# Per-row scale columns of two row tiles computed together on VectorE, in a gated cross-attention and bit-quantised FFN kernel

## The chip, the cores and the metric

The kernel runs on one core of a Trainium2 chip. The metric is the time of one execution on the device in microseconds (us), smaller is better. The profile's times are counted from the start of the execution's span.

## The reference

The input x has 32 batches of 224 rows of 512 elements, 7168 rows in all. Two gated residual blocks follow each other:

```python
x = x + tanh(g_xattn[0]) * xattn(layernorm(x), ctx, pad_mask, Wq, Wkv)
x = x + tanh(g_ffn[0]) * ffn(layernorm(x), w1, b1, w2, b2)

def rmsnorm(x):      return x * rsqrt(mean(x * x) + 1e-5)
def act_quant(x):    # per row
    scale = 127.0 / clip(max(abs(x)), 1e-5)
    return clip(round(x * scale), -128, 127) / scale
def weight_quant(w): # ternary, one scale for the whole matrix
    scale = 1.0 / clip(mean(abs(w)), 1e-5)
    return clip(round(w * scale), -1, 1) / scale
def bitlinear(x, w, b): return act_quant(rmsnorm(x)) @ weight_quant(w).T + b
ffn: bitlinear(gelu(bitlinear(x, w1, b1)), w2, b2)     # 512 -> 2048 -> 512
```

Each row of a layer's input so needs a handful of single numbers: its rms factor, its peak, the step with which it is quantised, and the factor that undoes the step after the matmul.

## The kernel before

The kernel has two stages in one launch. The first, until about 1587 us, is the cross-attention; it writes its rows to HBM. The second is the FFN, and only it is touched.

The second stage works on 56 row tiles of 128 rows (a row on each partition). Its steps are numbered s = -2 to 57, and a step works on several tiles at once: tile s goes through the first matmul, the GELU and its own quantisation (this is called **hidden**: its middle layer, 2048 columns in `hid`), tile s - 1 through the second matmul, and tile s + 2 is loaded, normalised and quantised (**ahead**: the input tile, 512 columns in `xc`). Steps 0 to 53 have both hidden and ahead. Steps -2 and -1 have ahead only, 54 and 55 hidden only. Steps 4 to 51 are a loop with four steps to a turn. Each engine has its own fixed order of instructions inside a step, and semaphores join them.

VectorE's order in a step: `L1007` (four pieces, matmul result times a column plus bias into `hid`), `L1011` and `L1014` (transposed tiles out of PSUM to bf16), `L1018`, `L1020`, `L1022` (mean and variance of tile s + 2), `L1026` (peak of `hid`, HMAX), `L1029` (HMS, from the sum of squares of ScalarE), `L1034` (peak of `xc`, XMAX), then eight small instructions on one column each, `L1039` to `L1060`, and `L1065`, which quantises `xc` into `xq`. The next step starts with `L1007` again.

The small instructions write columns of `cols`. For hidden they are HCLIP (L1039), HINV (L1048), HDEQ (L1053) and HS (L1055), for ahead XCLIP (L1044), XINV (L1051), XS (L1058) and XDEQ (L1060). Each `own_cols` wait makes VectorE wait for its own earlier result.

GpSimd's order in a step: `L928` and `L930` (x1 of tile s + 2 from x and the attention rows), `L916` (the final sum of tile s - 2), `L935` and `L938` (FAC, the factor of tile s + 2), `L943` (`xc`), `L947` (HR, the rms factor of tile s, after L1029), `L951` (x1 plus the bias of the second layer). In the trace L951 of one step is directly followed by L928, L930 and L916 of the next.

ScalarE's order: `L968` (GELU, four pieces), `L971` (transposed tile out of PSUM), `L976` (sum of squares), `L982` (the second matmul's result), `L985` (quantises `hid` with HS, waits for `t_hs`). TensorE's: `L1086` (first matmul, 16 matmuls), `L1094` (transposes `xq`, waits for `t_xq`), `L1103` (transposes the quantised hidden tile, waits for L985), `L1115` (second matmul, waits for L1014). SP issues the loads of a tile after `t_x1` (L930) and the store of a result after `t_yo` (L916).

Of the kernel before, what the change touches and what calls it, by code (L numbers as in the profile page):

```python
# [8 lines left out]
ALU = mybir.AluOpType  # L9
# [5 lines left out]
CLIP = 1e-5  # L15
LEVELS = 127.0
# [7 lines left out]
def gated_cross_attention_bit_ffn(nc, x, ctx_t, mask_row, mask_col, g_xattn, g_ffn,  # L24
# [32 lines left out]
    with outer:  # L57
        def sem(name):
            return outer.enter_context(nc.semaphore(name))

        def allocator(stack):
            return lambda name, shape, dt=F32: stack.enter_context(nc.sbuf_tensor(name, shape, dt))
# [11 lines left out]
        sb = allocator(outer)  # L74
        gates = sb("gates", [128, 2])
# [8 lines left out]
        w_mean = sb("w_mean", [128, 2])  # L84
# [6 lines left out]
        sb = allocator(phase_a)  # L91
# [724 lines left out]
        sb = allocator(phase_b)  # L816
        w1_q = sb("w1_q", [128, DC, F], BF16)
        w2_q = sb("w2_q", [128, FC, D], BF16)
        round_col = sb("round_col", [128, 2])
        w_gated = sb("w_gated", [128, 1])  # L820
        b1_row = sb("b1_row", [128, F])
        b2_row = sb("b2_row", [128, D])
        b2_gated = sb("b2_gated", [128, D])
# [2 lines left out]
        x1b = sb("x1b", [128, 2, D])  # L826
        xc = sb("xc", [128, 2, D])
        x_st, x_mv2 = sb("x_st", [128, 6]), sb("x_mv2", [128, 2, 2])
        cols = sb("cols", [128, 2, 16])
        xq = sb("xq", [128, 2, D])  # L830
        xq_t = sb("xq_t", [128, 2, DC * 128], BF16)
        hid = sb("hid", [128, 2, F])
# [1 line left out]
        hq = sb("hq", [128, 2, F])  # L834
        hq_t = sb("hq_t", [128, 2, FC * 128], BF16)
        yo = sb("yo", [128, 2, D])
        (NEGM, FVAR, FAC, XMAX, XCLIP, XINV, XS, XDEQ, HSS, HMS, HR, HMAX, HCLIP, HINV, HS, HDEQ) = range(16)


        halves = psum[:].bitcast(F16)  # L840
# [7 lines left out]
        b_const, b_wg, b_b2 = sem("b_const"), sem("b_wg"), sem("b_b2")  # L848
# [4 lines left out]
        t_g, t_ss, t_ms, t_hr, t_hs = sem("t_g"), sem("t_ss"), sem("t_ms"), sem("t_hr"), sem("t_hs")  # L853
        t_hq, t_ht, t_ha, t_hd = sem("t_hq"), sem("t_ht"), sem("t_ha"), sem("t_hd")
        t_y, t_ye, t_yo = sem("t_y"), sem("t_ye"), sem("t_yo")
        own_ab, own_fac, own_st, own_cols = sem("own_ab"), sem("own_fac"), sem("own_st"), sem("own_cols")

        def exists(k):
            return not isinstance(k, int) or 0 <= k < NT

        def is_step(s, n):
            return isinstance(s, int) and s == n

        def run_steps(eng, step):
            full = (NT - 2) // NX
            for s in range(-2, NX):
                step(s, s, 0)
            with eng.Fori(1, full) as u:
                for j in range(NX):
                    step(eng.snap(u * NX + j), j, u)  # L870
            for s in range(full * NX, NT + 2):
                step(s, s - full * NX, full)

        with nc.Block() as block:
# [80 lines left out]
            @block.scalar  # L955
            def _(act):
                act.wait_ge(b_const, 2)
                w2_flat = w2_q[:].rearrange("p c n -> p (c n)")

                def step(s, j, u):  # L960
                    c = cols[:, j % 2, :]
                    if is_step(s, 0):
                        act.activation(w2_flat, w_raw[:, DC * F:], ACT.Copy, bias=-ROUND).then_inc(b_wq2, 1)
                    if exists(s):
                        for i in range(FS):
                            seg = hid[:, j % 2, BANK * i:BANK * i + BANK]
                            act.wait_ge(t_he, FS * s + (i + 1))
                            act.activation(seg, seg, ACT.Gelu).then_inc(t_g, 1)  # L968
                    if exists(s - 1):
                        act.wait_ge(t_ht, 2 * s)  # L970
                        act.activation(hq_t[:, (j - 1) % 2, F // 2:], ps_ht[1], ACT.Copy, bias=-HALF_BIAS).then_inc(t_ha, 1)  # L971
                    if exists(s):
                        act.wait_ge(t_g, FS * s + FS)
                        if exists(s - 1):
                            act.wait_ge(t_ss, s)
                        act.activation(junk[:], hid[:, j % 2, :], ACT.Square, accum_out=c[:, HSS:HSS + 1]).then_inc(t_ss, 1)  # L976
                    if exists(s - 1):
                        p = (j - 1) % 2
                        act.wait_ge(t_y, s)
                        if exists(s - 3):  # L980
                            act.wait_ge(b_st[p], 16 * (2 * u + (j - 3) // 2 + 1))
                        act.activation(yo[:, p, :], ps_y, ACT.Copy, scale=cols[:, p, HDEQ:HDEQ + 1]).then_inc(t_ye, 1)  # L982
                    if exists(s):
                        act.wait_ge(t_hs, s + 1)
                        act.activation(hq[:, j % 2, :], hid[:, j % 2, :], ACT.Identity, scale=c[:, HS:HS + 1],  # L985
                                       bias=round_col[:, 1:2]).then_inc(t_hq, 1)

                run_steps(act, step)

            @block.vector  # L990
            def _(dve):
                dve.tensor_scalar(w1_q[:].rearrange("p c n -> p (c n)"), stage, ROUND, 1.0, ALU.subtract, ALU.mult).then_inc(b_wq1, 1)
                dve.tensor_tensor(w_gated[:], w_mean[:, 1:2], gates[:, 1:2], ALU.mult).then_inc(b_wg, 1)
                dve.wait_ge(b_wg, 1)

                def step(s, j, u):
                    c, slot = cols[:, j % 2, :], (j + 2) % NX
                    hidden, ahead = exists(s), exists(s + 2)
                    if is_step(s, 0):
                        dve.wait_ge(b_bias, 32)  # L1000
                    if hidden:
                        if exists(s - 2):
                            dve.wait_ge(t_hq, s - 1)
                        for i in range(FS):
                            dve.wait_ge(t_h, FS * s + (i + 1))
                            n = slice(BANK * i, BANK * i + BANK)
# [17 lines left out]
                    if hidden:  # L1024
# [2 lines left out]
                                          apply_absolute_value=True).then_inc(own_cols, 1)  # L1027
                        dve.wait_ge(t_ss, s + 1)
                        dve.tensor_scalar(c[:, HMS:HMS + 1], c[:, HSS:HSS + 1], 1.0 / F, RMS_EPS, ALU.mult, ALU.add).then_inc(t_ms, 1)  # L1029
                    h = 1 if hidden else 0  # L1030
                    x = 1 if ahead else 0
                    if ahead:
                        dve.wait_ge(t_xc, s + 3)
                        dve.tensor_reduce(c[:, XMAX:XMAX + 1], xc[:, j % 2, :], AX.X, ALU.max,  # L1034
                                          apply_absolute_value=True).then_inc(own_cols, 1)
                    if hidden:
                        dve.wait_ge(t_hr, s + 1)
                        dve.wait_ge(own_cols, h)
                        dve.tensor_scalar(c[:, HCLIP:HCLIP + 1], c[:, HMAX:HMAX + 1], c[:, HR:HR + 1], CLIP,  # L1039
                                          ALU.mult, ALU.max).then_inc(own_cols, 1)  # L1040
                    if ahead:
                        dve.wait_ge(t_fac, s + 3)
                        dve.wait_ge(own_cols, h + x)
                        dve.tensor_scalar(c[:, XCLIP:XCLIP + 1], c[:, XMAX:XMAX + 1], c[:, FAC:FAC + 1], CLIP,  # L1044
                                          ALU.mult, ALU.max).then_inc(own_cols, 1)
                    if hidden:
                        dve.wait_ge(own_cols, h + x + h)
                        dve.reciprocal(c[:, HINV:HINV + 1], c[:, HCLIP:HCLIP + 1]).then_inc(own_cols, 1)  # L1048
                    if ahead:
                        dve.wait_ge(own_cols, 2 * (h + x))  # L1050
                        dve.reciprocal(c[:, XINV:XINV + 1], c[:, XCLIP:XCLIP + 1]).then_inc(own_cols, 1)  # L1051
                    if hidden:
                        dve.tensor_scalar(c[:, HDEQ:HDEQ + 1], c[:, HCLIP:HCLIP + 1], 1.0 / LEVELS, w_gated[:], ALU.mult, ALU.mult)  # L1053
                        dve.wait_ge(own_cols, 2 * (h + x) + h)
                        dve.tensor_scalar(c[:, HS:HS + 1], c[:, HINV:HINV + 1], LEVELS, c[:, HR:HR + 1], ALU.mult, ALU.mult).then_inc(t_hs, 1)  # L1055
                    if ahead:
                        dve.wait_ge(own_cols, 3 * (h + x))
                        dve.tensor_scalar(c[:, XS:XS + 1], c[:, XINV:XINV + 1], LEVELS, c[:, FAC:FAC + 1],  # L1058
                                          ALU.mult, ALU.mult).then_inc(own_cols, 1)
                        dve.tensor_scalar(c[:, XDEQ:XDEQ + 1], c[:, XCLIP:XCLIP + 1], 1.0 / LEVELS, w_mean[:, 0:1],  # L1060
                                          ALU.mult, ALU.mult).then_inc(own_cols, 1)
                        if exists(s):
                            dve.wait_ge(t_xt, s + 1)
                        dve.wait_ge(own_cols, 3 * (h + x) + 1)
                        dve.tensor_scalar(xq[:, j % 2, :], xc[:, j % 2, :], c[:, XS:XS + 1], ROUND_HALF, ALU.mult, ALU.add).then_inc(t_xq, 1)  # L1065
                        dve.wait_ge(own_cols, 3 * (h + x) + 2)
                    if hidden or ahead:
                        dve.sem_clear(own_cols)

                run_steps(dve, step)  # L1070

            @block.tensor
# [76 lines left out]
```

## Time and profile before

| | |
|---|---|
| median of 3 runs | 2128.5 us (2127.22 to 2129.57) |
| the profiled execution | 2131.0 us |
| its span in the trace | 2129.2 us |
| TensorE busy | 1971.3 us, 93% |
| VectorE busy | 1236.9 us, 58% |
| ScalarE busy | 1060.9 us, 50% |
| GpSimd busy | 565.8 us, 27% |
| mean granted clock of TensorE | 0.981 |

The shares are means over both stages. In the page's 40 slices TensorE shows nines nearly throughout the first stage and eights in the last ten slices, where VectorE shows nines. What bounds the second stage has to be read from that stretch alone.

### The profile page before, as it was taken

To read this page: it belongs to the slowest core of one execution; us is meant where nothing else is said; L and a number is where in the kernel's file an instruction comes from. 1 tells how busy PE (TensorE), PEld (TensorE's weight loads), DVE (VectorE), ACT (ScalarE), POOL (GpSimd) and SP (SyncE) were. 2 spreads that over 40 slices of the span, in tenths; PEclk is the share of its full clock that TensorE was granted. 3 is DMA by queue.
4 is the path that set the end of the run, shared out by engine and by line. 5 is a ranking of instruction groups with operands and counts; after the bars stand their busy time and mean duration, and the time that the engine had idled before them with its cause. 6 is when DMAs were issued, how large, how long until landed. Compare 5 with 4: busy or idle time off the path is not lost. (4 is left out here: it accounts for less than half of the span.)

```text
span 2129.2 us, 47929 instructions
## 1 busy us (share of the span) xinstructions
PE 1971.3 (93%) x17116; PEld 1501.0 (70%) x17173; DVE 1236.9 (58%) x2371; ACT 1060.9 (50%) x1826; POOL 565.8 (27%) x619
## 2 busy tenths in 40 slices
PE   5999999999997999999999899999977888888887
PEld 4888888788886878888888688888763444444443
DVE  5455445444443444444544244444348999999996
ACT  2444433334333433333444244333346888888887
POOL 1111111111111111111111011111106777777774
PEclk9999999999998999999999899999998999999999
DMA  6000001021001003000000200001032222222221
GB/s 256 27 26 26 26 26 30 24 78 48 28 26 48 26 6 96 32 26 26 26 26 26 79 27 26 26 26 40 15 96 70 84 89 89 89 89 86 81 84 55
DMA packets 51968, 112.19 MB, mean 53 GB/s; under 512 B 5047, under 2 KB 5047, under 8 KB 51288
## 3 DMA queue, kind: packets, MB, share of 16 engines
q1 hardware_dynamic: 51928, 111.67, 15.9%
q8 instruction: 23, 0.38, 0.1%
q14 instruction: 17, 0.14, 0.0%
HBM read 93.36 MB, written 29.43 MB: 58 GB/s over the span
## 5 line engine op out<-in xcount | busy, mean ns | idle before, releaser
L316 POOL TENSOR_TENSOR y_l<-y,y_h 128x750 fp32r<-128x750 f32 x96 | 172.9, 1802 | 818.5 <-ACT y_h L378 818.1
L502 DVE TENSOR_REDUCE nmax<-psum 112x1 f32<-112x750 f32 x248 | 233.0, 939 | 164.3 <-PE psum L627 161.5
L400 ACT ACTIVATE prob<-psum,nmax 112x750 f32<-112x750 f32 x248 | 219.8, 886 | 92.8 <-DVE nmax L502 88.0
L1115 PE MATMUL psum<-w_q,hq_t 128*128 128x512 bf16 x841 | 194.5, 384 | 61.9 <-DVE hq_t L1014 61.9
L627 PE MATMUL psum<-y_h,wkv_h 128*128 128x512 f32 x756 | 208.4, 357 | 42.3 <-DVE wkv_l L465 14.0
L627 PE MATMUL psum<-wkv_h,y_h 128*125 128x512 f32 x558 | 226.6, 406 | 0.0
L721 PE MATMUL psum<-ident,prob 112*125 112x112 f32 x1488 | 214.9, 281 | 9.3 <-ACT prob_t L391 6.4
L627 PE MATMUL psum<-wkv_l,y_h 128*125 128x512 f32 x558 | 220.5, 395 | 0.0
L627 PE MATMUL psum<-wkv_h,y_l 128*125 128x512 f32 x558 | 220.4, 395 | 0.0
L1086 PE MATMUL psum<-w_q,xq_t 128*128 128x512 bf16 x895 | 204.6, 382 | 2.3 <-DVE xq_t L1011 2.3
L721 PEld LDWEIGHTS psum<-ident,prob 112*125 112x125 f32 x1488 | 181.3, 188 | 35.6 <-issue 22.8
L391 ACT ACTIVATE prob_t<-psum 125x336 f32<-125x336 f32 x248 | 111.2, 448 | 190.5 <-PE psum L721 190.4
L627 PE MATMUL psum<-y_l,wkv_h 128*128 128x512 f32 x756 | 196.6, 342 | 0.0
L627 PE MATMUL psum<-y_h,wkv_l 128*128 128x512 f32 x756 | 194.9, 340 | 0.0
L1115 PEld LDWEIGHTS psum<-w_q,hq_t 128*128 128x128 bf16 x896 | 84.5, 98 | 154.1 <-issue 63.8
L424 ACT ACTIVATE v<-psum 125x512 f32<-125x512 f32 x93 | 55.6, 597 | 247.8 <-PE psum L627 247.8
L524 DVE COPY prob_t<-psum 125x336 f32<-125x336 f32 x248 | 124.9, 504 | 75.4 <-PE psum L721 74.5
L1086 PEld LDWEIGHTS psum<-w_q,xq_t 128*128 128x128 bf16 x896 | 88.1, 98 | 109.4 <-issue 4.2
L627 PEld LDWEIGHTS psum<-y_h,wkv_h 128*128 128x128 f32 x756 | 116.7, 194 | 60.0 <-issue 38.3
L1007 DVE SCALAR_TENSOR_TENSOR hid<-psum,cols,b_row 128x512 f32<-128x512 f32 x224 | 152.7, 738 | 5.5 <-PE psum L1086 5.0
L321 POOL TENSOR_SCALAR x_var<-x_mv 56x1 f32<-56x1 f32 x31 | 5.7, 183 | 513.8 <-DVE x_mv L485 513.8
L627 PE MATMUL psum<-k_h,q_h 128*112 128x512 f32 x496 | 137.2, 357 | 4.4 <-issue 4.4
(122 smaller groups left out, 3651.0 us busy)
## 6 DMA issues: line engine op xcount, KB each, us to landing
y<-in_ctx_t SPq DMA_DIRECT2D x32, 1125.0 KB, 5.3
xb<-in_x SPq DMA_DIRECT2D x56, 256.0 KB, 2.7
ab<-attn_rows SPq DMA_DIRECT2D x56, 256.0 KB, 2.9
out_rows<-yo SPq DMA_DIRECT2D x56, 256.0 KB, 2.0
attn_rows<-vmean_rows SPq DMA_DIRECT2D x32, 336.0 KB
w_raw<-in_w_t SPq DMA_DIRECT2D x2, 4096.0 KB, 16.6
xa<-in_x SPq DMA_DIRECT2D x32, 112.0 KB
attn_rows<-attn SPq DMA_DIRECT2D x31, 112.0 KB
```

The costliest lines, as they stand in the source:

```text
L316: pool.tensor_tensor(y_l[:, c, :], y[:, c, :], y_h[:, c, :].bitcast(F32), ALU.subtract).then_inc(a_yl, 1)
L321: pool.tensor_scalar(x_var[:], x_mv[:, 1:2], 1.0, LN_EPS, ALU.mult, ALU.add).then_inc(own_var, 1)
L391: act.activation(prob_t[:, i % 2, 0:MH, :].rearrange("p j n -> p (j n)"), ps_pt[0], ACT.Copy).then_inc(p.pa, 1)
L400: act.activation(prob[:, i % 3, :], ps_score[i % 2][0:RP, :], ACT.Exp, bias=nmax[:, i:i + 1], accum_out=den[:, i:i + 1]).then_inc(p.exp, 1)
L424: act.activation(v[:, j, :], ps_v[0], ACT.Copy).then_inc(a_va, 1)
L502: dve.tensor_reduce(nmax[:, i:i + 1], ps_score[i % 2][0:RP, :], AX.X, ALU.max, negate=True).then_inc(p.max, 1)
L524: dve.tensor_copy(prob_t[:, i % 2, MH:MJ, :].rearrange("p j n -> p (j n)"), ps_pt[1]).then_inc(p.pd, 1)
L627: mm = pe.matmul(out[:, s0:s1], a, r[:, s0:s1], start=first and n == 0, stop=last_ and n == 2)
L721: mm = pe.transpose(ps_pt[hf][:, RP * j:RP * j + RP], prob[:, m % 3, MC * jj:MC * jj + MC], ident[0:RP, 0:RP])
L1007: dve.scalar_tensor_tensor(out=hid[:, j % 2, n], in0=psum[:, i, :], scalar=c[:, XDEQ:XDEQ + 1], in1=b1_row[:, n], op0=ALU.mult, op1=ALU.ad ...
L1086: mm = pe.matmul(psum[:, i, :], xq_t[:, j % 2, 128 * c:128 * c + 128], w1_q[:, c, BANK * i:BANK * i + BANK], start=(c == 0), stop=(c == DC ...
L1115: mm = pe.matmul(ps_y, hq_t[:, p, 128 * c:128 * c + 128], w2_q[:, c, :], start=(c == 0), stop=(c == FC - 1))
```

## The change

The small instructions of hidden and ahead are merged: the columns of both are laid side by side in `cols`, and five instructions work on two columns where eight worked on one. Their form changes with it. The factor of each row was a pointer scalar of a tensor_scalar; now products of two columns are a tensor_tensor with two inputs in SBUF. In steps with only one of the two, the same five instructions run on one column. The semaphore `t_hs` now counts every such step, so ScalarE waits for s + 3. The text calls the five RAW, QUANT, INV, DEQ and STEP, after what they write.

```diff
-        w_gated = sb("w_gated", [128, 1])
-        cols = sb("cols", [128, 2, 16])
+        cols = sb("cols", [128, 2, 18])
...
+        NEGM, FVAR, HSS, HMS = range(4)
+        HR, FAC, HMAX, XMAX, HS, XS, HDEQ, XDEQ = range(4, 12)
+        RMS, PEAK, STEP, DEQ, RAW, QUANT, INV = 4, 6, 8, 10, 12, 14, 16
+        w_pair = sb("w_pair", [128, 2])
...
-                        act.wait_ge(t_hs, s + 1)
+                        act.wait_ge(t_hs, s + 3)
...
-                dve.tensor_tensor(w_gated[:], w_mean[:, 1:2], gates[:, 1:2], ALU.mult).then_inc(b_wg, 1)
-                dve.wait_ge(b_wg, 1)
+                dve.tensor_tensor(w_pair[:, 0:1], w_mean[:, 1:2], gates[:, 1:2], ALU.mult).then_inc(b_wg, 1)
+                dve.tensor_copy(w_pair[:, 1:2], w_mean[:, 0:1]).then_inc(b_wg, 1)
+                dve.wait_ge(b_wg, 2)
...
                     if hidden:
                         dve.wait_ge(t_hr, s + 1)
-                        dve.wait_ge(own_cols, h)
-                        dve.tensor_scalar(c[:, HCLIP:HCLIP + 1], c[:, HMAX:HMAX + 1], c[:, HR:HR + 1], CLIP,
-                                          ALU.mult, ALU.max).then_inc(own_cols, 1)
                     if ahead:
                         dve.wait_ge(t_fac, s + 3)
...
+                    if hidden or ahead:
+                        h, x = 0 if hidden else 1, 2 if ahead else 1
+                        n = x - h
+                        dve.wait_ge(own_cols, n)
+                        dve.tensor_tensor(c[:, RAW + h:RAW + x], c[:, PEAK + h:PEAK + x], c[:, RMS + h:RMS + x],
+                                          ALU.mult).then_inc(own_cols, 1)
+                        dve.wait_ge(own_cols, n + 1)
+                        dve.tensor_scalar(c[:, QUANT + h:QUANT + x], c[:, RAW + h:RAW + x], CLIP, 1.0 / LEVELS,
+                                          ALU.max, ALU.mult).then_inc(own_cols, 1)
+                        dve.wait_ge(own_cols, n + 2)
+                        dve.reciprocal(c[:, INV + h:INV + x], c[:, QUANT + h:QUANT + x]).then_inc(own_cols, 1)
+                        dve.tensor_tensor(c[:, DEQ + h:DEQ + x], c[:, QUANT + h:QUANT + x], w_pair[:, h:x],
+                                          ALU.mult).then_inc(own_cols, 1)
+                        dve.wait_ge(own_cols, n + 3)
+                        dve.tensor_tensor(c[:, STEP + h:STEP + x], c[:, INV + h:INV + x], c[:, RMS + h:RMS + x],
+                                          ALU.mult).then_inc(t_hs, 1)
                     if ahead:
...
                         if exists(s):
                             dve.wait_ge(t_xt, s + 1)
-                        dve.wait_ge(own_cols, 3 * (h + x) + 1)
+                        dve.wait_ge(t_hs, s + 3)
                         dve.tensor_scalar(xq[:, j % 2, :], xc[:, j % 2, :], c[:, XS:XS + 1], ROUND_HALF, ALU.mult, ALU.add).then_inc(t_xq, 1)
-                        dve.wait_ge(own_cols, 3 * (h + x) + 2)
                     if hidden or ahead:
+                        dve.wait_ge(own_cols, n + 4)
                         dve.sem_clear(own_cols)
```

The other seven small instructions of before (L1044 to L1060) go in the same way as L1039.

## Rows read from the trace of the kernel before

**Rows 1.** Busy time of each engine in the even stretch of the second stage.
```profile
1700.00:2100.00 400.00, 350.30 (x2245) 187.25 (x2287) 391.40 (x924) 337.92 (x397) 288.85 (x352) 1.00 0.25 85
```

**Rows 2.** Timeline of TensorE: start, length, line, shape, count, [idle before, releaser].
```profile
1903.57 3.40 PE L1115 MATMUL psum<-w_q,hq_t 128*128 128x512 bf16 x15 [1.38 <-DVE hq_t L1014]
1906.81 3.62 PE L1086 MATMUL psum<-w_q,xq_t 128*128 128x512 bf16 x16
...
1912.60 3.40 PE L1115 MATMUL psum<-w_q,hq_t 128*128 128x512 bf16 x15 [1.06 <-DVE hq_t L1014]
```

**Rows 3.** Timeline of VectorE around the edited piece of one step.
```profile
1906.44 0.68 DVE L1034 TENSOR_REDUCE cols<-xc 128x1 f32<-128x512 f32 x1
1907.19 0.21 DVE L1039 TENSOR_SCALAR cols<-cols 128x1 f32<-128x1 f32 x1
...
1908.18 0.49 DVE L1065 TENSOR_SCALAR xq<-xc,cols 128x512 f32<-128x512 f32 x1
1908.60 1.40 DVE L1007 SCALAR_TENSOR_TENSOR hid<-psum,cols,b_row 128x512 f32<-128x512 f32 x2
```

**Rows 4.** Timelines of GpSimd and VectorE in steps -2 and -1.
```profile
1599.23 1.26 POOL L930 TENSOR_TENSOR x<-xb,ab 128x512 f32<-128x512 f32 x1
...
1605.51 0.69 POOL L928 TENSOR_SCALAR ab<-ab,gates 128x512 f32<-128x512 f32 x1 [0.23 <-POOL b_gated L909]
...
1600.00 0.78 DVE L1065 TENSOR_SCALAR xq<-xc,cols 128x512 f32<-128x512 f32 x1
...
1604.65 0.69 DVE L1034 TENSOR_REDUCE cols<-xc 128x1 f32<-128x512 f32 x1 [1.74 <-POOL xc L943]
1605.44 0.21 DVE L1044 TENSOR_SCALAR cols<-cols 128x1 f32<-128x1 f32 x1
1605.69 0.16 DVE L1051 RECIPROCAL cols<-cols 128x1 f32<-128x1 f32 x1
...
1606.14 0.48 DVE L1065 TENSOR_SCALAR xq<-xc,cols 128x512 f32<-128x512 f32 x1
```

**Rows 5.** Groups of small VectorE forms: count, busy us, mean ns, idle before.
```profile
L487 DVE TENSOR_TENSOR x_keep<-x_rstd,mcol 56x1 f32<-56x1 f32 x31 | 4.7, 152 | 36.3 <-POOL x_rstd L323 36.3
...
L1029 DVE TENSOR_SCALAR cols<-cols 128x1 f32<-128x1 f32 x56 | 8.1, 144 | 1.0 <-ACT junk L976 1.0
```

**Rows 6.** Timeline of GpSimd in the same step as rows 3.
```profile
1906.60 0.55 POOL L947 TENSOR_TENSOR cols<-cols,half 128x1 f32<-128x1 f32 x1 [0.69 <-DVE cols L1029]
1907.12 1.27 POOL L951 TENSOR_TENSOR x1b<-x,b_gated 128x512 f32<-128x512 f32 x1
1908.37 0.86 POOL L928 TENSOR_SCALAR ab<-ab,gates 128x512 f32<-128x512 f32 x1
1909.31 1.28 POOL L930 TENSOR_TENSOR x<-xb,ab 128x512 f32<-128x512 f32 x1
1910.55 1.30 POOL L916 TENSOR_TENSOR yo<-yo,x1b 128x512 f32<-128x512 f32 x1
```

**Rows 7.** First stage: L465 on VectorE (timeline, group) and GpSimd's timeline.
```profile
11.87 2.06 DVE L465 TENSOR_TENSOR wkv_l<-w_raw,wkv_h 128x1536 fp32r<-128x1536 f32 x1 [11.75 <-ACT wkv_h L360]
...
L465 DVE TENSOR_TENSOR wkv_l<-w_raw,wkv_h 128x1536 fp32r<-128x1536 f32 x2 | 3.7, 1901 | 11.7 <-ACT wkv_h L360 11.7
...
8.81 3.50 POOL L316 TENSOR_TENSOR y_l<-y,y_h 128x750 fp32r<-128x750 f32 x2
```

**Rows 8.** Timelines of VectorE and GpSimd at the second stage's start.
```profile
1589.21 4.43 DVE L992 TENSOR_SCALAR w_q<-w_raw 128x8192 bf16<-128x8192 f32 x1 [2.57 <-PEq L221]
1593.55 0.15 DVE L993 TENSOR_TENSOR w_gated<-w_mean,gates 128x1 f32<-128x1 f32 x1
...
1592.89 1.31 POOL L928 TENSOR_SCALAR ab<-ab,gates 128x512 f32<-128x512 f32 x1 [3.60 <-DMA ab<-attn_rows]
```

**Rows 9.** TensorE after a wait in the first stage, and the granted clock (last but two).
```profile
418.73 4.43 PE L796 MATMUL psum<-wv,y_sum 128*8 128x512 f32 x6 [2.03 <-DVE y_sum L603]
...
419.00:423.00 4.00, 4.00 (x6) 0.50 (x4) 0.00 (x0) 0.00 (x0) 0.00 (x0) 0.57 0.00 0
```

More of the change, by code:

```diff
@@ L836, in gated_cross_attention_bit_ffn @@
         yo = sb("yo", [128, 2, D])
-        (NEGM, FVAR, FAC, XMAX, XCLIP, XINV, XS, XDEQ, HSS, HMS, HR, HMAX, HCLIP, HINV, HS, HDEQ) = range(16)
+        NEGM, FVAR, HSS, HMS = range(4)
+        HR, FAC, HMAX, XMAX, HS, XS, HDEQ, XDEQ = range(4, 12)
+        RMS, PEAK, STEP, DEQ, RAW, QUANT, INV = 4, 6, 8, 10, 12, 14, 16
+        w_pair = sb("w_pair", [128, 2])
         halves = psum[:].bitcast(F16)
@@ L1029, in step @@
                         dve.tensor_scalar(c[:, HMS:HMS + 1], c[:, HSS:HSS + 1], 1.0 / F, RMS_EPS, ALU.mult, ALU.add).then_inc(t_ms, 1)
-                    h = 1 if hidden else 0
-                    x = 1 if ahead else 0
                     if ahead:
@@ L1037, in step @@
                         dve.wait_ge(t_hr, s + 1)
-                        dve.wait_ge(own_cols, h)
-                        dve.tensor_scalar(c[:, HCLIP:HCLIP + 1], c[:, HMAX:HMAX + 1], c[:, HR:HR + 1], CLIP,
-                                          ALU.mult, ALU.max).then_inc(own_cols, 1)
                     if ahead:
                         dve.wait_ge(t_fac, s + 3)
-                        dve.wait_ge(own_cols, h + x)
-                        dve.tensor_scalar(c[:, XCLIP:XCLIP + 1], c[:, XMAX:XMAX + 1], c[:, FAC:FAC + 1], CLIP,
-                                          ALU.mult, ALU.max).then_inc(own_cols, 1)
@@ L1046, in step @@
-                    if hidden:
-                        dve.wait_ge(own_cols, h + x + h)
-                        dve.reciprocal(c[:, HINV:HINV + 1], c[:, HCLIP:HCLIP + 1]).then_inc(own_cols, 1)
-                    if ahead:
[L1050 to L1061, printed above, removed]
+                    if hidden or ahead:
[14 more added lines that the diff above has]
+                                          ALU.mult).then_inc(t_hs, 1)
```

## The prediction, made before the change was run

> **What bounds the kernel now.** I read the page first for the shares, then the busy times of the long even stretch, then the timelines of single engines through one step, and last the odd places where a VectorE and a GpSimd instruction meet. In the even stretch from 1700 to 2100 us VectorE is busy 391.4 of 400 us and TensorE 350.3 [rows 1], at full granted clock. The second stage repeats every 9.03 us, as the two starts of the L1115 group show (1903.57 and 1912.60), and each time TensorE waits 1.06 to 1.38 us for VectorE's L1014 [rows 2]. So VectorE's chain of instructions sets the period, and what the change does to it counts 54 times (the steps that have both a hidden tile and a tile two ahead), with two half steps at each end.
>
> All times below without the 19 in front are of the step shown: 7.19 is 1907.19. The piece that is edited runs from L1039 at 7.19 to the start of L1065 at 8.18: eight small instructions in 0.99 us, 0.12 each [rows 3]. They need not wait for each other, since hidden and ahead alternate. L1065 writes xq and ends at 8.67; L1007, the next step's first, starts at 8.60.
>
> **The change on an idle chip.** It removes eight small instructions and adds five: RAW, QUANT, INV, DEQ and STEP. DEQ and INV follow QUANT without a wait between them; all the others wait for the one before. In the half steps a waiting instruction starts 0.04 after the end of what it waits for (L1044 ends at 5.65, L1051 starts at 5.69), and 0.10 after where the instruction has two waits (L1034 ends at 5.34, L1044 starts at 5.44) [rows 4]. The small forms take 0.144 (two immediates) and 0.152 (tensor_tensor) [rows 5], a reciprocal 0.16 [rows 4]. RAW starts 0.10 after the end of L1034, which is 7.12, so at 7.22 instead of 7.19 (it has three waits, one more than that pair of rows shows, so up to another 0.06 is possible). Then RAW to QUANT 0.19, QUANT to INV 0.18, INV to STEP 0.20, and STEP to L1065 0.25 (two waits): L1065 would start at 8.04 to 8.08 instead of 8.18, 0.10 to 0.14 earlier. TensorE could follow that only in part: the L1086 group ends at 10.43 [rows 2], and the fourth piece of L1007, 0.66 us apart from its neighbours, starts at 8.60 + 1.98 = 10.58 [rows 3]. That is 0.1 of slack once the handoff is paid. The wait that ScalarE's L985 has on STEP would end where it ends now. No DMA and no queue is moved: SP waits for t_x1 and t_yo, both GpSimd's. The 0.1 per step would be 6 us in all. I don't believe in it, for the reason that follows.
>
> **What GpSimd does meanwhile.** As soon as L947 is through, GpSimd starts L951, a tensor_tensor on 512 columns, at 7.12 and is in it until 8.39; then L928 (8.37), L930 (9.31) and L916 (10.55) follow without a pause [rows 6]. The whole edited piece lies beside L951, and now costs nothing of it. But some VectorE instructions can't run beside a GpSimd one. In step -2, L1065 starts at 1600.00 while GpSimd's L930 (1599.23 for 1.26) is in flight, and takes 0.78; in step -1 it takes 0.48 [rows 4]. The long one ends 0.29 after L930's end at 1600.49, so it was held until GpSimd had finished, and only then read its columns. Of the 0.48, then, 0.20 go by before the columns and 0.28 over them. The same is seen with a tensor_tensor of two SBUF inputs: the first L465 starts at 11.87 while L316 runs until 8.81 + 3.50 = 12.31, and takes 2.06, where its twin takes 2 x 1.901 - 2.06 = 1.74; it ends 1.62 after L316, which is its 1536 columns at 1.05 ns [rows 7]. Of its time 0.13 go by before the columns.
>
> In the shown step L1065 ends at 8.67, and 8.39 + 0.28 is 8.67 [rows 3, 6]: today it is already held, by a hair, to the end of L951. GpSimd is held in turn: L928 takes 0.86 instead of the 0.69 of [rows 4], ending 0.56 after L1065's end. So moving L1065's start forward gains nothing; its end stays at 8.67 unless L951 ends earlier, and L951 hangs on L1029 and L947, which the edit leaves alone. The gain above falls to zero.
>
> **What the new instructions cost there.** The old small ones have one column, a pointer scalar or immediates, and one tensor input; L1039 shows 0.21 beside L951 and the eight fit into 0.99, so there is no hold. The new RAW, DEQ and STEP are tensor_tensor with two SBUF inputs, like L465. RAW would start at 7.22 and want its columns at 7.35; L951 has been in since 7.12, so RAW is held until 8.39 and ends at 8.41. What that hold is worth for two columns no row shows. From below it is nothing: L993, one column, two SBUF inputs, took 0.152 at 1593.55, while L928, held by L992 until 1593.64, ended at 1594.20, the same 0.56 after [rows 8]. But L993 began while VectorE itself still had what L928 waited for. From above it is L465's full hold. I take the hold, since the kind is L465's and the overlap here is clean: GpSimd is in first by 0.10.
>
> QUANT has one tensor input, but two columns where all the old ones had one. L1065's 512 columns go by in 0.28, 0.55 ns each against 1.05 for L465, so that form reads two columns at once, and it was held. [...] Bounds: not held like L1029 (0.144), or held like L1065. I take held. [...]
>
> The order of events, with each side starting as today after what it follows: QUANT starts at 8.45, but L928 has been in since 8.37 and needs 0.69, so until 9.06; QUANT ends at 9.08. INV runs from 9.12 to 9.28. DEQ starts at 9.20 and wants its columns at 9.33; L930 starts 0.08 after L928, at 9.14, and is in until 10.41; DEQ ends at 10.43. STEP starts 0.08 before that (as neighbours do), wants its columns at 10.48, and L916 starts at 10.37 and, by the same 0.14 that L928 shows (0.69 - 0.56), at 10.51: STEP just gets in and ends at 10.50. L1065 starts at 10.60 and is held by L916 to 10.37 + 1.28 = 11.65; it ends at 11.93 instead of 8.67. That is **3.26 us per step**. If STEP comes too late by the 0.03, it ends at 11.67, L1065 starts at 11.77 and ends at 12.25: 3.58. If DEQ comes before L930, STEP is held instead, and the end is the same to 0.1. I take 3.3. The period becomes 12.3 us. After L1065 everything follows as today: L985 starts near 10.55 instead of 7.99 and still ends before L1014; TensorE has its L1115 and L1086 done early and waits for xq, then for L1014.
>
> Sum: 54 x 3.3 = 178 us. The half steps at the start add some 0.9 (RAW held to 1600.49 in step -2), the two last ones at most a L951 and most of a L916 each, together 3.5, since STEP there feeds L985 directly. 182 us on the profiled execution's 2131.0 is 2313. That execution is 2.5 us above the median of 2128.5, so the forecast is **2310 us**.
>
> **Rivals.** (a) QUANT is not held, the tensor_tensors are. Then QUANT ends at 8.60, INV at 8.80, DEQ is held by L928 to 9.08, STEP gets in before L930 and ends at 9.15, and L1065, started at 9.26, is held by L930 to 10.41 and ends at 10.69: 2.0 per step, 54 x 2.0 + 4 = 112, so 2241. For it: every old small tensor_scalar ran free. Against: none had two columns.
>
> (b) Only QUANT is held, the small tensor_tensors are not (L993's reading). QUANT ends at 8.41, STEP at 8.80, L1065 starts at 8.91, gets in before L930 and ends at 9.39: 0.72 per step, 39 us, 2167.
>
> (c) Not slower: nothing as small as two columns is held, as L993 was not. Then L1065 is ready at 8.08 and still held to 8.39 by L951: the end stays 8.67 and the time 2128. It decides if the two-column instructions show 0.15 and not 1.2 beside L951.
>
> (d) Faster: nothing is held, L1065 neither, and the 0.1 of TensorE's slack is taken: 2122. Against it stands L1065's end at L951's end + 0.28. [...]
>
> (e) TensorE loses its clock. [...]
>
> **How the numbers follow.** Forecast 0.60, (a) 0.14, (b) 0.08, (c) 0.07, (d) 0.03, (e) 0.06, anything else 0.02. The forecast's own range is 2290 to 2345: 3.0 to 3.9 per step. The range 2160 to 2350 takes in (a) and (b) and leaves out (c), (d) and (e), 0.18. What a measurement can tell from no change is 0.2%, 4.3 us: faster 0.03, same 0.07, slower 0.90.
>
> **What would show it.** Right: the first tensor_tensor takes about 1.2 us and ends with L951; L1065 ends near a GpSimd end + 0.28 or runs after L916; the period is near 12.3; GpSimd's own times stay. If QUANT shows 0.15 it is (a); if the tensor_tensors show 0.15 it is (b) or (c). Wrong in size: the 0.03 us races at STEP and DEQ, and GpSimd starting in another order once VectorE is late.

## The result and the profile after

The changed kernel takes **2300.6 us** (median of 4 runs, 2298.6 to 2303.8); the kernel before took 2127.9 us (4 runs) beside it. The ratio is 1.082, with a 95% interval of 1.0806 to 1.0834. The forecast was 2310, the range 2160 to 2350. The change makes the kernel 8% slower.

Lines have moved: L1034 is now L1036, L1065 (xq) L1062, L1007 L1011, L985 L988; on GpSimd L947 is L950, L951 (x1b) L954, L928 L931, L930 L933, L916 L919. The five new instructions are RAW L1046, QUANT L1049, INV L1052, DEQ L1053 and STEP L1056.

The timeline of VectorE in one step of the changed kernel, with its next L1011, answers to [rows 3]:

```profile
1907.13 0.68 DVE L1036 TENSOR_REDUCE cols<-xc 128x1 f32<-128x512 f32 x1
1907.94 1.16 DVE L1046 TENSOR_TENSOR cols<-cols 128x2 f32<-128x2 f32 x1
1909.13 0.64 DVE L1049 TENSOR_SCALAR cols<-cols 128x2 f32<-128x2 f32 x1
1909.81 0.17 DVE L1052 RECIPROCAL cols<-cols 128x2 f32<-128x2 f32 x1
1909.89 1.22 DVE L1053 TENSOR_TENSOR cols<-cols,w_pair 128x2 f32<-128x2 f32 x1
1911.03 0.15 DVE L1056 TENSOR_TENSOR cols<-cols 128x2 f32<-128x2 f32 x1
1911.29 1.32 DVE L1062 TENSOR_SCALAR xq<-xc,cols 128x512 f32<-128x512 f32 x1
1912.53 2.71 DVE L1011 SCALAR_TENSOR_TENSOR hid<-psum,cols,b_row 128x512 f32<-128x512 f32 x4
```

And the timeline of GpSimd in the same step, to [rows 6]:

```profile
1907.30 0.55 POOL L950 TENSOR_TENSOR cols<-cols,half 128x1 f32<-128x1 f32 x1 [0.69 <-DVE cols L1033]
1907.81 1.27 POOL L954 TENSOR_TENSOR x1b<-x,b_gated 128x512 f32<-128x512 f32 x1
1909.06 0.69 POOL L931 TENSOR_SCALAR ab<-ab,gates 128x512 f32<-128x512 f32 x1
1909.83 1.26 POOL L933 TENSOR_TENSOR x<-xb,ab 128x512 f32<-128x512 f32 x1
1911.05 1.27 POOL L919 TENSOR_TENSOR yo<-yo,x1b 128x512 f32<-128x512 f32 x1
```

Read the two side by side, adding start and length. RAW ends at 9.10, x1b (L954) at 9.08. QUANT ends at 9.77, L931 at 9.75. DEQ ends at 11.11, L933 at 11.09. STEP gets in between L933 and L919 and takes its plain 0.15. xq ends at 12.61, 0.29 after L919's 12.32. Four of these six instructions (RAW, QUANT, DEQ and xq) end 0.02 or 0.29 after a GpSimd instruction, so most of their long durations must be waiting; the experiments below show it. No column of the view names GpSimd as the releaser: it isn't a semaphore that is waited for, and the time is booked as VectorE busy. So the page of the changed kernel shows VectorE busier, 1402.3 us against 1236.9, with fewer instructions, 2214 against 2371:

```profile
PE 2055.8 (89%) x17172; PEld 1515.9 (66%) x17173; DVE 1402.3 (61%) x2214; ACT 1081.7 (47%) x1826; POOL 554.4 (24%) x619
```

The groups of VectorE by shape in the second stage of the changed kernel (columns as in [rows 5]) show that this is so in all 54 steps with both halves:

```profile
L1062 DVE TENSOR_SCALAR xq<-xc,cols 128x512 f32<-128x512 f32 x56 | 71.6, 1279 | 5.9
L1053 DVE TENSOR_TENSOR cols<-cols,w_pair 128x2 f32<-128x2 f32 x54 | 65.1, 1205 | 0.0
L1046 DVE TENSOR_TENSOR cols<-cols 128x2 f32<-128x2 f32 x54 | 62.3, 1155 | 7.2
L1049 DVE TENSOR_SCALAR cols<-cols 128x2 f32<-128x2 f32 x54 | 35.2, 651 | 1.9
L1052 DVE RECIPROCAL cols<-cols 128x2 f32<-128x2 f32 x54 | 9.0, 166 | 1.8
L1056 DVE TENSOR_TENSOR cols<-cols 128x2 f32<-128x2 f32 x54 | 8.0, 148 | 0.0
```

The reciprocal is the only one of the five that is never held, and STEP arrives at the right moment. STEP can be held too: in step -1 of the run with half of x1b, below, it took 0.52 and ended 0.01 after GpSimd's instruction. Whether the reciprocal is free or only lucky in its moment, these rows alone don't say.

### The profile page after: what moved, and what is told of

Same layout as the page of the kernel before. It is cut to its first block and busy times, and to the rows that moved or that the text cites. A ratio compares the mean times of both kernels' runs of the same rounds, so it can differ in the third digit from the quotient of the medians.

```text
span 2302.0 us, 47774 instructions
## 1 busy us (share of the span) xinstructions
PE 2055.8 (89%) x17172; PEld 1515.9 (66%) x17173; DVE 1402.3 (61%) x2214; ACT 1081.7 (47%) x1826; POOL 554.4 (24%) x619
## 5 line engine op out<-in xcount | busy, mean ns | idle before, releaser
L1112 PE MATMUL psum<-w_q,hq_t 128*128 128x512 bf16 x896 | 258.7, 454 | 91.5 <-DVE hq_t L1018 91.5
L1112 PEld LDWEIGHTS psum<-w_q,hq_t 128*128 128x128 bf16 x896 | 97.5, 113 | 235.8 <-issue 175.4
L1083 PE MATMUL psum<-w_q,xq_t 128*128 128x512 bf16 x896 | 206.2, 384 | 3.2 <-DVE xq_t L1015 3.2
L988 ACT ACTIVATE hq<-hid,round_col,cols 128x2048 f32<-128x2048 f32 x56 | 117.3, 2095 | 101.2 <-DVE cols L1056 101.0
L1083 PEld LDWEIGHTS psum<-w_q,xq_t 128*128 128x128 bf16 x896 | 88.5, 99 | 111.6 <-issue 5.8
L1011 DVE SCALAR_TENSOR_TENSOR hid<-psum,cols,b_row 128x512 f32<-128x512 f32 x224 | 152.1, 737 | 0.2
L971 ACT ACTIVATE hid<-hid 128x512 f32<-128x512 f32 x224 | 139.8, 629 | 16.9 <-DVE hid L1011 12.2
```

Source lines behind the costliest of these rows:

```text
L1011: dve.scalar_tensor_tensor(out=hid[:, j % 2, n], in0=psum[:, i, :], scalar=c[:, XDEQ:XDEQ + 1], in1=b1_row[:, n], op0=ALU.mult, op1=ALU.ad ...
L1083: mm = pe.matmul(psum[:, i, :], xq_t[:, j % 2, 128 * c:128 * c + 128], w1_q[:, c, BANK * i:BANK * i + BANK], start=(c == 0), stop=(c == DC ...
L1112: mm = pe.matmul(ps_y, hq_t[:, p, 128 * c:128 * c + 128], w2_q[:, c, :], start=(c == 0), stop=(c == FC - 1))
```

## The experiments

In each diff the kernel it starts from is named. Between them these runs had 63 runs of the kernel before beside them, with medians of 2127.6, 2126.6 and 2126.5 us in the three sets.

**QUANT on one column at a time.** From the changed kernel:

```diff
-  dve.tensor_scalar(c[:, QUANT + h:QUANT + x], c[:, RAW + h:RAW + x], CLIP, 1.0 / LEVELS, ALU.max, ALU.mult).then_inc(own_cols, 1)
+  for i in range(h, x):
+      q = dve.tensor_scalar(c[:, QUANT + i:QUANT + i + 1], c[:, RAW + i:RAW + i + 1], CLIP, 1.0 / LEVELS, ALU.max, ALU.mult)
+  q.then_inc(own_cols, 1)
```

> Only QUANT is changed: two instructions on one column each in the place of one on two. Theory (hold: a VectorE instruction with two SBUF inputs, or with one SBUF input that can be split in two, waits until the GpSimd instruction in flight has ended): QUANT now shows 0.15 us, RAW stays near 1.15, DEQ is held by the short GpSimd L931 only, STEP gets in before L933, and xq ends with L933 instead of L919, so 2.0 us per step over the kernel before instead of 3.25: 2237 us. Rival (chain: the five are slow because each waits for the one before, whatever GpSimd does): one instruction more in the chain, so no faster than the changed kernel, 2300 us or a few more.

Measured: 2235.7 us, ratio 1.0507 (1.0491 to 1.0523). One instruction more makes the kernel 65 us faster, so the length of the chain is not what costs. The timeline of VectorE, with its x1b ending at 1913.74:

```profile
1912.60 1.16 DVE L1046 TENSOR_TENSOR cols<-cols 128x2 f32<-128x2 f32 x1
1913.79 0.21 DVE L1050 TENSOR_SCALAR cols<-cols 128x1 f32<-128x1 f32 x2
1914.04 0.17 DVE L1054 RECIPROCAL cols<-cols 128x2 f32<-128x2 f32 x1
```

The two one-column QUANTs run together in 0.21 while GpSimd's L931 is in flight (1913.71 to 1914.41); on two columns the same work took 0.64. The reciprocal on two columns lies wholly beside L931 too and takes its 0.17, so on two columns the tensor_scalar was held (0.64) and the reciprocal was not (0.17).

**All five on one column at a time.** From the changed kernel, each line of the five becomes a loop over the columns (ten instructions), for example:

```diff
-  dve.tensor_tensor(c[:, RAW + h:RAW + x], c[:, PEAK + h:PEAK + x], c[:, RMS + h:RMS + x], ALU.mult).then_inc(own_cols, 1)
+  for i in range(h, x):
+      dve.tensor_tensor(c[:, RAW + i:RAW + i + 1], c[:, PEAK + i:PEAK + i + 1], c[:, RMS + i:RMS + i + 1], ALU.mult).then_inc(own_cols, 1)
```

> The changed kernel with each of the five done on one column at a time (ten instructions), products still with two SBUF inputs. Theory (hold, whatever the number of columns): the first RAW is held about 1.15 us to the end of the GpSimd x1b instruction, QUANT runs free (one column can't be split), the first DEQ is held by the short GpSimd instruction; then the last STEP and GpSimd's next come to within 0.02 us of each other: 2236 if STEP is first, 2302 if not. Rival (one column is too little to be held, as L993 seemed to show): everything free and xq held to the end of x1b as before, 2128 to 2135.

Measured: 2235.0 us, ratio 1.0512 (1.0496 to 1.0528); the last STEP came in time. The two RAWs and the two QUANTs here, with x1b ending at 1909.85:

```profile
1908.71 1.23 DVE L1048 TENSOR_TENSOR cols<-cols 128x1 f32<-128x1 f32 x2
1909.90 0.22 DVE L1052 TENSOR_SCALAR cols<-cols 128x1 f32<-128x1 f32 x2
```

The first RAW waits for x1b and the second stands behind it. One column was enough for the hold with two SBUF inputs (1.23 for the two RAWs), and not with one (0.22 for the two QUANTs). The changed kernel shows it by itself in its two last steps, where only hidden is left and the same instruction has one column (the two steps are alike); its timelines of VectorE and GpSimd:

```profile
2274.88 1.21 DVE L1046 TENSOR_TENSOR cols<-cols 128x1 f32<-128x1 f32 x1 [0.66 <-POOL cols L950]
2276.12 0.15 DVE L1049 TENSOR_SCALAR cols<-cols 128x1 f32<-128x1 f32 x1
...
2274.81 1.26 POOL L954 TENSOR_TENSOR x1b<-x,b_gated 128x512 f32<-128x512 f32 x1
```

**Only QUANT left exposed.** From the changed kernel; peak and INV go to a free part of PSUM, a copy of w_pair too, so that each product has one input there:

```diff
+  pcols = psum[:, 7, 256:272].rearrange("p (a b) -> p a b", a=2)      # p = pcols[:, j % 2, :]
+  w_psum = psum[:, 7, 272:274]
+  dve.tensor_copy(w_psum, w_pair[:])
-  dve.tensor_tensor(c[:, RAW + h:RAW + x], c[:, PEAK + h:PEAK + x], c[:, RMS + h:RMS + x], ALU.mult)
+  dve.tensor_tensor(c[:, RAW + h:RAW + x], p[:, P_PEAK + h:P_PEAK + x], c[:, RMS + h:RMS + x], ALU.mult)
   dve.tensor_scalar(c[:, QUANT + h:QUANT + x], c[:, RAW + h:RAW + x], CLIP, 1.0 / LEVELS, ALU.max, ALU.mult)
-  dve.reciprocal(c[:, INV + h:INV + x], c[:, QUANT + h:QUANT + x])
+  dve.reciprocal(p[:, P_INV + h:P_INV + x], c[:, QUANT + h:QUANT + x])
```

DEQ and STEP change in the same way.

> The two-column chain in which only QUANT has its input and output in SBUF and two columns; each product has one of its inputs in PSUM. Theory (hold by the form that takes two columns at once): QUANT is held to the end of x1b and takes near 1.1 us, the others 0.15 to 0.2, xq starts 0.7 us later than before, gets in ahead of the next but one GpSimd instruction and ends 0.73 later per step: 2167 us. Rival (only two SBUF inputs are held): 2126, as with all in PSUM.

Measured: 2166.0 us, ratio 1.0185 (1.017 to 1.0201). GpSimd's x1b runs from 1907.00 to 1908.26 in this step of VectorE's timeline:

```profile
1907.13 0.16 DVE L1052 TENSOR_TENSOR cols<-psum,cols 128x2 f32<-128x2 f32 x1
1907.33 0.97 DVE L1055 TENSOR_SCALAR cols<-cols 128x2 f32<-128x2 f32 x1
1908.33 0.17 DVE L1058 RECIPROCAL psum<-cols 128x2 f32<-128x2 f32 x1
```

The product that was held for 1.16 takes 0.16 beside the same x1b, and QUANT takes the wait on itself. That is the price of QUANT alone, 39 us. It is also what rival (b) had worked out for a kernel in which only QUANT is held, 2167.

**None exposed.** The same, with RAW and QUANT in PSUM too (and w_pair back in SBUF, since DEQ's other input now lies in PSUM):

```diff
-  dve.tensor_scalar(c[:, QUANT + h:QUANT + x], c[:, RAW + h:RAW + x], CLIP, 1.0 / LEVELS, ALU.max, ALU.mult)
+  dve.tensor_scalar(p[:, P_QUANT + h:P_QUANT + x], p[:, P_RAW + h:P_RAW + x], CLIP, 1.0 / LEVELS, ALU.max, ALU.mult)
```

> The same five instructions on two columns with the same waits, but peak, RAW, QUANT and INV lie in a free part of PSUM, so none has two SBUF inputs or an SBUF input to split. Theory (hold): all five show 0.15 to 0.20 us, xq starts 0.1 us earlier than in the kernel before and is still held to the end of the GpSimd x1b instruction, so the period is 9.03 us again: 2128 us, within 3. Rival (chain): the five stay at about 3.2 us beyond before, 2300. Rival (the hold of xq is no hold but chance): xq ends 0.1 earlier and the time is 2122.

Measured: 2125.9 us, ratio 0.9995 (0.9986 to 1.0004). Same five instructions, same waits, same two columns, and 175 us less. Its timelines of VectorE and GpSimd:

```profile
1910.33 0.17 DVE L1049 TENSOR_TENSOR psum<-psum,cols 128x2 f32<-128x2 f32 x1
...
1911.21 0.54 DVE L1065 TENSOR_SCALAR xq<-xc,cols 128x512 f32<-128x512 f32 x1
...
1910.20 1.26 POOL L956 TENSOR_TENSOR x1b<-x,b_gated 128x512 f32<-128x512 f32 x1
```

xq starts 0.05 earlier in the step than in [rows 3] and takes 0.54 instead of 0.49: it ends at 11.75, where x1b's 11.46 + 0.28 says. The time gained ahead of it is gone in it, as the prediction said of the kernel before.

**x1b behind xq, in both kernels.** One wait of GpSimd moves, from both kernels:

```diff
-  pool.wait_ge(t_xq, s + 1)
+  if exists(s + 2):
+      pool.wait_ge(t_xq, s + 3)      # xq of this step
+  else:
+      pool.wait_ge(t_hs, s + 3)      # s + 1 in the kernel before
   ...
   pool.tensor_tensor(x1b[:, j % 2, :], x1[:, j % NX, :], b2_gated[:], ALU.add).then_inc(t_x1b, 1)
```

> The changed kernel with one wait of GpSimd moved: its x1b instruction, and with it the three that follow, waits until xq of this step is written (in the two last steps until STEP is). Nothing on VectorE is changed. Theory (hold): RAW, QUANT, DEQ and STEP show 0.15 us, xq shows 0.49 and ends 0.1 to 0.15 us earlier in the step than before, TensorE becomes the bound at a period near 8.93: 2122 us, between 2119 and 2127. Rival (chain): 2300, since VectorE's order and waits are the same. Rival (GpSimd late): the three GpSimd instructions now end 1.2 us later and hold up the next step's statistics, which would show as VectorE waiting for x1: over 2135.

> The kernel before with the same GpSimd wait moved. Theory (hold): only xq was held there, by 0.01 us, and nothing else of VectorE is touched, so the period stays 9.03: 2128 us within 2. It gives what the moved wait costs or gives by itself, to be taken off the run beside it. Rival: if the moved wait by itself helps, 2122 here too; if GpSimd comes late, over 2135.

Measured: the changed kernel with it 2123.0 us, ratio 0.9984 (0.9974 to 0.9993); the kernel before with it 2128.5, ratio 0.9998 (0.9989 to 1.0007). VectorE's timeline in the changed kernel with x1b late:

```profile
1909.32 0.68 DVE L1039 TENSOR_REDUCE cols<-xc 128x1 f32<-128x512 f32 x1
1910.13 0.16 DVE L1049 TENSOR_TENSOR cols<-cols 128x2 f32<-128x2 f32 x1
1910.33 0.17 DVE L1052 TENSOR_SCALAR cols<-cols 128x2 f32<-128x2 f32 x1
1910.53 0.17 DVE L1055 RECIPROCAL cols<-cols 128x2 f32<-128x2 f32 x1
1910.62 0.14 DVE L1056 TENSOR_TENSOR cols<-cols,w_pair 128x2 f32<-128x2 f32 x1
1910.73 0.16 DVE L1059 TENSOR_TENSOR cols<-cols 128x2 f32<-128x2 f32 x1
1911.00 0.49 DVE L1065 TENSOR_SCALAR xq<-xc,cols 128x512 f32<-128x512 f32 x1
```

Nothing of VectorE was edited, and everything is back to 0.14 to 0.17. The two together say that the change is worth some 4 to 5 us once GpSimd is out of its way, and that the moved wait alone is worth nothing. The period here is 8.95 instead of 9.02 us, which over 54 steps is 4 us. With both remedies the result should not be better than with one:

> Both remedies together: the five with PSUM inputs, and x1b after xq. Theory: neither is needed once the other is there, so the same as the changed kernel with x1b late, or 1 to 2 us slower, since the PSUM forms showed 0.17 to 0.18 instead of 0.15 to 0.17: 2123 to 2126. Rival (the remedies add up): under 2121.

Measured: 2123.4 us, ratio 0.9989 (0.998 to 0.9998), period 8.98. They don't add up.

**How long x1b is.** Two tests of the dose. From the changed kernel, x1b on half its columns (its other half is filled with zeros once, so this kernel leaves half of the residual out of its result):

```diff
-  pool.tensor_tensor(x1b[:, j % 2, :], x1[:, j % NX, :], b2_gated[:], ALU.add)
+  pool.tensor_tensor(x1b[:, j % 2, 0:D // 2], x1[:, j % NX, 0:D // 2], b2_gated[:, 0:D // 2], ALU.add)
```

> The changed kernel with x1b done on 256 of its 512 columns (the other half of the residual is left out of the result). Theory: RAW is held to an end that comes 0.57 us earlier (256 columns at 2.2 ns), and everything behind it, GpSimd's and VectorE's, moves with it: 2300.6 - 54 x 0.57 = 2270 us. Rival (the wait is for something else, and x1b's length is nothing to VectorE): 2300.

Measured: 2269.7 us, ratio 1.0676 (1.0659 to 1.0692), where 2270 was expected. The period fell by 0.54 and not by 0.57, to 11.73, so that the two agree to the microsecond is partly chance. VectorE's and GpSimd's timelines:

```profile
1904.45 0.62 DVE L1047 TENSOR_TENSOR cols<-cols 128x2 f32<-128x2 f32 x1
...
1904.32 0.72 POOL L955 TENSOR_TENSOR x1b<-x,b_gated 128x256 f32<-128x256 f32 x1
```

On the kernel before, the first try was to do x1b twice:

```diff
+  pool.tensor_tensor(x1b[:, j % 2, :], x1[:, j % NX, :], b2_gated[:], ALU.add).then_inc(own_fac, 1)
+  pool.wait_ge(own_fac, 1)
   pool.tensor_tensor(x1b[:, j % 2, :], x1[:, j % NX, :], b2_gated[:], ALU.add).then_inc(t_x1b, 1)
+  pool.sem_clear(own_fac)
```

> The kernel before with GpSimd's x1b instruction done twice in a row (the second writes the same again). Theory (xq of the kernel before is already held to the end of x1b): each step grows by the whole second instruction, 1.24 us, though GpSimd is busy only seven tenths of the time: 54 x 1.24 = 67, 2195 us. Rival (GpSimd's idle time is free; xq and x1b only happen to end in step): GpSimd has 1.6 us to spare ahead of the statistics, so 2128.

Measured: 2125.9 us, ratio 0.9995 (0.9985 to 1.0006). The expectation was wrong, and the rival's 2128 was right in number. The timelines of VectorE and GpSimd say why, and that the rival's reason doesn't follow from it:

```profile
1905.46 0.49 DVE L1068 TENSOR_SCALAR xq<-xc,cols 128x512 f32<-128x512 f32 x1
...
1904.40 1.27 POOL L951 TENSOR_TENSOR x1b<-x,b_gated 128x512 f32<-128x512 f32 x1
1905.75 1.35 POOL L953 TENSOR_TENSOR x1b<-x,b_gated 128x512 f32<-128x512 f32 x1
```

The second x1b waits for the first and starts 0.08 us after it. By then xq, already waiting, has gone in, and now it is GpSimd that is held, for 1.35 instead of 1.27. Here it is the instruction in flight that holds (xq 0.49 with the first x1b ended), and not the work that GpSimd has still to do. The test of the dose must move the end of the one in flight, so a small instruction was put ahead of it:

```diff
   pool.tensor_tensor(c[:, HR:HR + 1], c[:, HMS:HMS + 1], half[:], ALU.pow).then_inc(t_hr, 1)
+  pool.tensor_scalar(spare[:], ident[:], 1.0, 1.0, ALU.mult, ALU.mult).then_inc(own_fac, 1)
+  pool.wait_ge(own_fac, 1)
+  pool.sem_clear(own_fac)
```

> The kernel before with one small GpSimd instruction more (128 columns, into a spare tile) ahead of x1b, so that x1b starts and ends about 0.35 us later; unlike the doubled x1b, whose start fell behind xq's, x1b itself is still the one in flight when xq wants its columns. Theory (xq of the kernel before ends with x1b + 0.28): each step grows by 0.34, 54 x 0.34 = 18, 2145 us. Rival (xq isn't held in the kernel before, GpSimd's idle time covers it): 2127.

Measured: 2151.3 us, ratio 1.0116 (1.01 to 1.0131), 6 us above the expectation. The timelines:

```profile
1907.15 1.04 DVE L1069 TENSOR_SCALAR xq<-xc,cols 128x512 f32<-128x512 f32 x1
...
1906.10 0.30 POOL L949 TENSOR_SCALAR spare<-ident 128x128 f32<-128x128 f32 x1
1906.64 1.27 POOL L955 TENSOR_TENSOR x1b<-x,b_gated 128x512 f32<-128x512 f32 x1 [0.24 <-POOL spare L949]
```

xq ends at 8.19 and x1b at 7.91, again 0.28 apart. The dose was larger than planned: between the small instruction and x1b GpSimd idles 0.24, so x1b starts 1.07 after L948's start where [rows 6] have 0.52, 0.55 later. 0.55 over 54 steps is 30 us. Some 4 of them come back: in the kernel before, each of the eleven steps in which the loop turns is 0.33 us longer than the others, and here all are 9.58, as if the turn lay inside the hold. So GpSimd, busy 27% of the span, was on the critical path of the kernel before, level with VectorE's own chain: x1b later costs time at once, and x1b out of the way (2128.5) gains none.

**The last wait.** From the changed kernel with x1b late:

```diff
-                    if ahead:
-                        dve.wait_ge(t_fac, s + 3)
```

> The changed kernel with x1b late and without VectorE's wait for FAC ahead of RAW, which the earlier wait for xc already implies. Theory: RAW starts 0.10 after the reduction instead of 0.13, the period falls from 8.95 by what TensorE lets through, 0.02 to 0.03: 2121 to 2122 us. Rival (TensorE already sets 8.95): no change from 2123.

Measured: 2121.9 us, ratio 0.9985 (0.9976 to 0.9995). The wait could go because GpSimd writes xc after FAC, and VectorE has already waited for xc. In the profile the period is 8.93 instead of 8.95, as expected, which is 1 us in all. The medians of the two kernels, from different sets, can't tell them apart (single executions of this one went from 2119.9 to 2127.2). Both are faster than the kernel before, by 0.15%, and nearly 8% faster than the changed one.

## Why the prediction was right

**What bounds the stage.** VectorE's chain: nearly the whole slowdown is found between L1036 and L1011 of each step (5.40 us apart in the step shown, 2.16 in [rows 3]). The first L1036 of a step with both halves starts 0.84 us later than its counterpart in the kernel before, the next 53 steps take 165.3 us more, and what follows the last one 6.6 more. That makes 172.8 in all, the difference of the spans.

**The order of events.** The times worked out in the prediction, against the step shown, both counted from the start of the reduction of xc (L1034, now L1036):

| | predicted | measured |
|---|---|---|
| RAW starts | 0.78 | 0.81 |
| RAW ends (with x1b) | 1.97 | 1.97 |
| QUANT ends (with L931) | 2.64 | 2.64 |
| DEQ ends (with L933) | 3.99 | 3.98 |
| STEP ends (in between) | 4.06 | 4.05 |
| xq ends (with L919) | 5.49 | 5.48 |

xq ended at 2.23 in the kernel before, so the step costs 3.25; 3.26 was worked out and 3.3 taken. The period is 12.27 in most steps. STEP's place ahead of L919 rested on a margin of 0.03 us, and the group's mean of 148 ns shows that it held in all 54 steps. Had it failed, the prediction's 3.58 a step would have made some 17 us more, still inside the range. The experiments give the parts a price: QUANT alone 39 us, everything but QUANT 108, nothing exposed 0. These don't add up to 173, since each instruction that is held pushes the next ones into other GpSimd instructions: with QUANT alone xq gets in freely, with QUANT split it ends with L933, in the changed kernel with L919.

**The choice between the bounds.** L993 was read as the lower bound, and the one-column RAW of the last steps and of the ten-instruction run shows that a single column is no protection. That fits the doubt stated in the prediction: L993 began at 1593.55, while VectorE's own L992 ran to 1593.64 and L928 took 1.31 beside it instead of 0.69 [rows 8, 4]; no run tests L993 itself. That L1065's form reads two columns at once was the author's estimate, from 0.55 ns a column against 1.05, and no run shows how a column is read. The runs show that QUANT was held with its two columns in SBUF (0.64, and 0.97 with the products free), and was free one column at a time (0.21 for both) and with its two columns in PSUM (0.17). Rivals (b) and (c) fall with RAW's 1.16. Rival (a) fell with QUANT's 0.64, and the run with QUANT split, 2235.7, is near what (a) had worked out for a kernel in which QUANT is free, 2241. Rival (d) falls with the run in PSUM: with no instruction of the five held, xq still ends with x1b and nothing is gained. Its 2122 is what came of it once x1b was out of xq's way too, 2123.

**What was sized too large.** The sum said 182 us, the median moved by 172.7. The start (0.84 against 0.9) and the end (6.6, of which 3.25 are the last full step's, against 3.5) were right. 3.3 for 3.25 is 2.7 us. The rest is in the 54 equal steps that aren't equal. The third full step of the kernel before was 2.5 us longer than the others: L1007 waited for TensorE, whose L1115 just before it took 5.86 where it takes 3.40 in [rows 2]. The changed kernel has no such step. The loop's turn made eleven steps 0.33 longer before, 3.6 us in all, and shows in no step after. Two of the first steps of the changed kernel are shorter than 12.27, by 1.4 together. Against that, five of its steps are longer, by 1.0 together, for a reason told below. No term of the sum had these; together with the 2.7 they make 9.2 us, nearly the whole difference.

**The gain on an idle chip** was put at 0.10 to 0.14 per step of VectorE and is 0.07 (9.02 to 8.95): RAW starts 0.13 after the reduction, not 0.10, with its three waits, and QUANT on two columns takes 0.17, not 0.144. The run without the wait for FAC gives 0.02 of it back.

**TensorE's clock**, which the chance of (e) stands for, did fall, in nearly every second step, and most of the loss stayed hidden. The busy times of the changed kernel's even stretch give a granted clock of 0.89 (last but two), against 1.00 in [rows 1]. In the step shown L1112 takes 4.98 for its 16 matmuls, where it takes 3.61 in the steps on either side:

```profile
1700.00:2200.00 500.00, 385.84 (x2114) 183.18 (x2113) 484.62 (x736) 329.72 (x367) 257.92 (x324) 0.89 0.19 65
```

```profile
1904.05 4.98 PE L1112 MATMUL psum<-w_q,hq_t 128*128 128x512 bf16 x16 [1.81 <-DVE hq_t L1018]
1908.86 3.62 PE L1083 MATMUL psum<-w_q,xq_t 128*128 128x512 bf16 x16
1912.66 0.40 PE L1091 MATMUL psum<-ident_h,xq 128*128 128x128 f16 x4 [0.18 <-DVE xq L1062]
```

L1083 still ends at 12.48, before xq at 12.61. Without the 1.37 us lost (4.98 less 3.61), TensorE would have waited 1.5 us ahead of L1091. The prediction's times come to the same: 11.93 for the end of xq less 10.43 for the end of L1086 is 1.5. The lost clock did not carry the time past 2350, beyond which (e) lay: the longest step with both halves took 12.54.

In five of the 54 steps the loss is larger and is not hidden. The timelines of TensorE, ScalarE, GpSimd and VectorE in one of them, and TensorE's next L1112:

```profile
1805.65 6.37 PE L1112 MATMUL psum<-w_q,hq_t 128*128 128x512 bf16 x16 [1.81 <-DVE hq_t L1018]
1812.15 0.69 ACT L985 ACTIVATE yo<-psum,cols 128x512 f32<-128x512 f32 x1 [4.12 <-PE psum L1112]
1812.92 1.27 POOL L919 TENSOR_TENSOR yo<-yo,x1b 128x512 f32<-128x512 f32 x1 [0.23 <-ACT yo L985]
1812.89 1.59 DVE L1062 TENSOR_SCALAR xq<-xc,cols 128x512 f32<-128x512 f32 x1
1818.19 3.61 PE L1112 MATMUL psum<-w_q,hq_t 128*128 128x512 bf16 x16 [1.60 <-DVE hq_t L1018]
```

From 1805.92 to 1811.90 the granted clock is 0.55, and [rows 9] have 0.57 in the 4 us after a wait of 2.03; in the next L1112 it is 1.00, though TensorE had waited before both (1.81 and 1.60). L985 takes the result of L1112 and comes late, L919 waits for L985, and xq is held to the end of L919: 1.59 instead of 1.32, and the step takes 12.54. The five steps lose 1.0 us together. The prediction did not have this way from TensorE's clock through ScalarE and GpSimd to VectorE.

**What was held, over all runs.** Beside GpSimd's instructions a tensor_tensor with two SBUF inputs was held down to one column (RAW on one column took 1.21 us beside x1b), and so was a tensor_scalar from SBUF to SBUF on two columns (0.64) and on 512 (xq, 1.32). In the steps shown the small ones ended 0.01 to 0.04 and xq 0.28 or 0.29 after GpSimd's. The number of chained instructions was no guide here. Where the hold decides, ten instructions took 65 us less than five; where it is out of the way, three instructions fewer gained 0.07 us a step (9.02 to 8.95) and not 0.36, three at 0.12 each, because each of the new ones waits for the one before.

## What to carry to other kernels

Before merging small VectorE instructions, write down for each new one how many inputs it has in SBUF and how many columns, and look at what GpSimd has in flight at that place: in this kernel a pointer scalar with one column ran free (0.21 us), and so did a reciprocal on two columns (0.17). A tensor_tensor with a second SBUF input waited for the end of GpSimd's instruction even on one column (1.21), and a tensor_scalar on two columns of SBUF did too (0.64). In these profiles such a wait has no releaser and counts as busy (1402.3 us of VectorE against 1236.9); it is found where a duration differs between instances of one shape (1.16 and 0.16) and ends fall on the other engine's ends. The cures that worked here are to move one input of a product to PSUM (for the tensor_scalar, its input and its output; 2125.9 us), or to let GpSimd wait until the chain is through (2123.0). Only then did this merge show what it is worth, some 4 to 5 us.

## What the runs showed of the hardware that was not expected

The end of the hold is sharp here: in the traces of four kernels (the changed one, QUANT split, only QUANT, half of x1b) a small held instruction ends within 0.04 us of GpSimd's end, and where xq is held it ends 0.27 to 0.30 after it, so an order of events with a margin of 0.03 us could be worked out ahead. A waiting VectorE instruction went into a gap of 0.08 us between two dependent GpSimd instructions, and a second instruction that GpSimd had still to do cost it nothing (xq 0.49, 2125.9 us in all).

The gap between two GpSimd instructions of which the second waits for the first is 0.08 us between L928 and L930 [rows 6] and between the two x1b, but 0.24 in the run with the small instruction, where a sem_clear and two more waits stand between them in the code. [rows 4] show 0.23 between L909 and L928, where another wait and a sem_inc stand between them. Which of them takes the time isn't shown.

The turn of a loop, 0.33 us where VectorE's chain set the period, does not show where the engine was held in every step: in the changed kernel and in the two tests of the dose, the steps with a turn are as long as their neighbours (12.27, 11.73 and 9.58).
